# A hybrid scan and attention block: dt spread over the state groups by repeating transfers

## The reference, cut to what matters

```python
def _selective_scan(xc, dt, Bmat, Cmat, A, D):
    def step(h, inp):
        dt_t, B_t, C_t, x_t = inp
        dA = jnp.exp(dt_t[..., None] * A)                 # decay
        dBx = dt_t[..., None] * B_t[:, None, :] * x_t[..., None]   # drive = (dt * x) * B
        h = dA * h + dBx                                  # scan
        y = jnp.einsum('bdn,bn->bd', h, C_t)              # read and fold
        return (h, y)
    ...
    return jnp.swapaxes(ys, 0, 1) + xc * D

dt = jax.nn.softplus(dt_low @ W_dt + b_dt)
y = _selective_scan(xh, dt, Bmat, Cmat, A, D)
y = y * jax.nn.silu(z)
...                       # W_out, group norm, silu, + x
t = t + _L1_attn_ref(_ln_t(t), ...)      # 8 heads, 1024 x 1024 causal in the kernel's tiling
t = t + _L1_ffn_ref(_ln_t(t), ...)       # 8 experts, top 2
```

## Time and profile before

| | |
|---|---|
| median of 3 runs | 1569.61 us (1568.96 to 1571.73) |
| profiled execution, first to last instruction | 1566.7 us |
| busy: PE, DVE, ACT, POOL | 1124.4, 1171.5, 703.5, 512.5 us |
| turn 1, ring | about 73 to 146 us |
| turn 2, ring | about 200 to 274 us |
| turn 3, ring | 343 to 427 us |
| turns 4 to 8 | 427 to 1280 us, 170.6 us each |
| turns 9 to 11 | 1280 to 1567 us |

### The profile page before, as it was taken

One profiled execution on the slowest core, in us unless ns is written; L12 is line 12 of the kernel. 1 busy time (PEld: TensorE's weight loads), 2 busy tenths in 40 slices (PEclk: granted clock), 3 DMA queues, 4 the chain that ended last, 5 costly groups with the idle time before them and its releaser, 6 DMA issues. The chain is left out here.

```text
span 1566.7 us, 17517 instructions
## 1 busy us (share of the span) xinstructions
PE 1124.4 (72%) x6288; PEld 459.2 (29%) x6388; DVE 1171.5 (75%) x1391; ACT 703.5 (45%) x1298; POOL 512.5 (33%) x272
## 2 busy tenths in 40 slices
PE   1444344778877887679767887778767977796794
PEld 0111111332233333333233332333333323343342
DVE  5198189788678887788788976888778879448445
ACT  0422432337633763366534763366435651470560
POOL 2354544244424432533334432353243331000000
PEclk9666656979987899879987999789986998698995
DMA  1200150020212012111202012201212120111000
GB/s 27 60 1 14 32 111 0 21 70 1 56 41 70 1 32 65 32 45 32 52 20 70 14 24 65 72 1 31 52 25 52 32 52 8 30 32 44 3 14 7
DMA packets 25965, 55.28 MB, mean 35 GB/s; under 512 B 8582, under 2 KB 8970, under 8 KB 23499
## 3 DMA queue, kind: packets, MB, share of 16 engines
q1 hardware_dynamic: 25878, 54.15, 15.2%
HBM read 28.54 MB, written 13.00 MB: 27 GB/s over the span
## 5 line engine op out<-in xcount | busy, mean ns | idle before, releaser
L671 POOL TENSOR_TENSOR read<-state,c_rep 128x1024 f32<-128x1024 f32 x128 | 304.3, 2378 | 458.4 <-DVE state L981 430.9
L937 DVE TENSOR_REDUCE row_max<-ps 128x1 f32<-128x768 f32 (+7 forms) x384 | 349.1, 950 | 95.4 <-PE ps L1213 93.2
L812 ACT ACTIVATE probs<-ps 128x512 f32<-128x512 f32 (+3 forms) x768 | 329.4, 497 | 136.4 <-PE ps L1316 82.9
L981 DVE TENSOR_TENSOR_SCAN state<-decay,drive 128x1024 f32<-128x1024 f32 x128 | 356.6, 2786 | 1.8 <-POOL read L671 1.1
L1209 PE MATMUL ps<-k_stack,q_stack 128*128 128x512 bf16 (+3 forms) x736 | 219.7, 379 | 106.8 <-DVE row_max L937 89.2
L990 DVE TENSOR_TENSOR drive<-ps,b_rep 128x512 f32<-128x512 f32 x256 | 169.5, 676 | 105.0 <-PE ps L1247 102.2
L1313 PE MATMUL ps<-q_stack,k_stack 128*128 128x512 bf16 (+3 forms) x734 | 208.5, 343 | 38.3 <-DVE drive L990 20.0
L773 ACT ACTIVATE decay<-ps,a_scale 128x512 f32<-128x512 f32 x256 | 175.2, 696 | 117.1 <-DVE state L981 101.5
L1328 PE MATMUL ps<-probs,v_aug 128*32 128x512 f32 (+3 forms) x1536 | 169.3, 513 | 5.5 <-ACT probs L812 1.8
L1247 PE MATMUL ps<-dt_rows,pick 128*128 128x512 bf16 x224 | 103.6, 462 | 93.1 <-DVE drive L990 73.8
L1247 PE MATMUL ps<-u_rows,pick 128*128 128x512 bf16 x254 | 116.8, 460 | 47.7 <-DMA u_rows<-read 17.8
(11 more groups left out here) (172 smaller groups left out, 1236.4 us busy)
## 6 DMA issues: line engine op xcount, KB each, us to landing
q_stack<-q_parts_dram SPq DMA_DIRECT2D x48, 192.0 KB
k_stack<-k_parts_dram SPq DMA_DIRECT2D x48, 192.0 KB
dt_rows<-read SPq DMA_DIRECT2D x96, 64.0 KB, 2.0
u_rows<-read SPq DMA_DIRECT2D x96, 64.0 KB, 2.0
k_parts_dram<-read SPq DMA_DIRECT2D x40, 128.0 KB, 2.4
q_parts_dram<-read SPq DMA_DIRECT2D x24, 128.0 KB, 2.3
xs<-in_x SPq DMA_DIRECT2D x8, 256.0 KB, 3.6
residual<-in_x SPq DMA_DIRECT2D x8, 256.0 KB, 9.2
```

The costliest lines, as they stand in the source:

```text
L671: pool.tensor_tensor(read[:, k % (2 * NG), :], state[:, k % 2, :], c_rep[:, :], ALU.mult)\
L812: act.activation(probs[:, e % (2 * QUAD), 0:w], bank_of(("scores", e))[:, 0:w], ACT.Exp, scale=SCALE).then_inc(exped.sem, 1)
L937: dve.tensor_reduce(row_max[:, i, h0:h0 + nh], scores[:, :, 0:P * (i + 1)], AX.X, ALU.max, negate=True).then_inc(row_maxed.sem, 1)
L981: dve.tensor_tensor_scan(state[:, k % 2, :], decay[:, k % 2, :], drive[:, k % 3, :], 0.0, ALU.mult, ALU.add).then_inc(scanned.sem, 1)
```

## The change

dt is no longer split and replicated on PE. SP stores dt in memory (`dt_dram`, one slot per image) and reads the 8 rows of a chunk back 16 times over, once for each state, into one of two slots of `dt_spread`. ACT takes the exponential of a whole chunk of 1024 tokens from there (`decay_chunk`). The first two spreads stand ahead of u's rows on SP, the next eleven behind the row maxima, and the last three between the two groups of stacks. u keeps its three parts and its matmuls. On ACT the B copy moves ahead of the logarithm and of the group norm. The tables `UNITS_IN`, `FOLDS` and `TURNS` have a few other numbers.

```diff
-        UNITS_IN = (2, 2, 2, 1, 0, 2, 2, 0, 2, 1, 2, 1, 1, 1, 2, 1, 0, 0, 1, 1, 2, 1, 1, 2, 0, 1, 0, 1)
-        FOLDS = ((0, 0, 13), (0, 1, 13), (1, 0, 18), (1, 1, 19))
+        UNITS_IN = (2, 2, 2, 1, 0, 2, 2, 0, 2, 1, 2, 1, 1, 1, 2, 0, 0, 1, 1, 1, 2, 1, 1, 2, 0, 1, 0, 1)
+        FOLDS = ((0, 0, 12), (0, 1, 13), (1, 0, 16), (1, 1, 21))
...
+        SPREAD_FIRST = 13
...
-                    users += [(kind, k2) for k2 in units[:1] for kind in ("dt", "u")]
+                    users += [("u", k2) for k2 in units[:1]]
...
+                    def spread_dt(first, last):
+                        for k in range(first, last):
+                            if k < 2:
+                                sp.wait_ge(dt_stored.sem, dt_stored.at(c, 16))
+                            else:
+                                sp.wait_ge(decayed.sem, decayed.at(c, k - 1))
+                            hold(sp, "sp")
+                            rows = dt_dram[c.number, CH * chunk(k)[2]:CH * (chunk(k)[2] + 1), :]
+                            sp.dma_start(dt_spread[:, k % 2, :], rows.unsqueeze(0).to_broadcast([NS, CH, T]))\
+                              .then_inc(dt_spread_in[k % 2].sem, 16)
+
                     if c:
-
-                        for r, parts in enumerate((high_parts, mid_parts, low_parts)):
-                            for n, (rows, arrived) in enumerate(((dt_rows, dt_rows_in), (u_rows, u_rows_in))):
-                                sp.wait_ge(parts.sem, parts.at(c, n + 1))
-                                hold(sp, "sp")
-                                for g in range(NG):
-                                    sp.dma_start(rows[32 * r:32 * (r + 1), g, :],
-                                                 part[3 * n + r][GW * g:GW * (g + 1), :]).then_inc(arrived.sem, 16)
+                        sp.wait_ge(dt_ready.sem, dt_ready.at(c, 1))
+                        hold(sp, "sp")
+                        sp.dma_start(dt_dram[c.number, :, :], dt).then_inc(dt_stored.sem, 16)
+                        spread_dt(0, 2)
+                        for r, part_ready in enumerate((high_part, mid_part, low_part)):
+                            sp.wait_ge(part_ready.sem, part_ready.at(c, 1))
+                            hold(sp, "sp")
+                            for g in range(NG):
+                                sp.dma_start(u_rows[32 * r:32 * (r + 1), g, :],
+                                             part[r][GW * g:GW * (g + 1), :]).then_inc(u_rows_in.sem, 16)
...
+                    if c:
+                        spread_dt(2, SPREAD_FIRST)
                     if p:
-
                         sp.wait_ge(qk_parts_out.sem, qk_parts_out.at(p, 16 * 8))
                         hold(sp, "sp")
-                        for quad in range(2):
+                    for quad in range(2):
+                        if quad and c:
+                            spread_dt(SPREAD_FIRST, NJ)
+                        if p:
...
-                    for batch, work in ((c, silu_argument), (c, gate_tanh), (c, softplus_start), (p, group_norm),
-                                        (c, softplus_end), (c, take_b), (c, lambda: high(0)), (c, take_c),
-                                        (p, take_t1), (p, take_xn_t), (c, lambda: high(1)), (c, lambda: mid(0)),
-                                        (p, high_qk), (c, lambda: mid(1)), (p, mid_qk)):
+                    for batch, work in ((c, silu_argument), (c, gate_tanh), (c, softplus_start), (c, take_b),
+                                        (c, softplus_end), (p, group_norm), (c, take_c), (c, high_u), (p, take_t1),
+                                        (c, mid_u), (p, take_xn_t), (p, high_qk), (p, mid_qk)):
...
-                    def decay_unit(k2):
-
-                        k, h = k2 // 2, k2 % 2
-                        act.wait_ge(dt_rep.sem, dt_rep.at(c, k2 + 1))
+                    def decay_chunk(k):
+
+                        arrived = dt_spread_in[k % 2]
+                        act.wait_ge(arrived.sem, arrived.at(c, 16 * (k // 2 + 1)))
                         if k >= 2:
                             act.wait_ge(scanned.sem, scanned.at(c, k - 1))
+                        else:
+                            act.wait_ge(low_part.sem, low_part.at(c, 1))
                         j = chunk(k)[2]
-                        act.activation(decay[:, k % 2, halves(h)], bank_of(("dt", k2)), ACT.Exp,
-                                       scale=a_scale[:, j:j + 1])\
-                           .then_inc(decayed.sem, 1)
+                        act.activation(decay[:, k % 2, :], dt_spread[:, k % 2, :], ACT.Exp,
+                                       scale=a_scale[:, j:j + 1]).then_inc(decayed.sem, 1)
...
-                        if k2 == 0:
-                            pe.wait_ge(dt_rows_in.sem, dt_rows_in.at(c, 16 * 3 * NG))
-                            pe.wait_ge(c_copied.sem, c_copied.at(c, 1))
-                        replicate(k2, free_bank(("dt", k2)), dt_rows).then_inc(dt_rep.sem, 1)
```

93 lines of the change are left out of this document (44 added, 49 removed).

## The result

The changed kernel takes 1532.13 us (median of 4 runs, 1526.7 to 1541.07), the kernel before 1569.55 beside it; the ratio is 0.977 (95% interval 0.975 to 0.979). It is 37 us faster. The forecast was 1504 with a range of 1475 to 1540: the sign and the range held, but only 37 of 65 us came.

The account below looks back on a forecast made before the run. Handovers between engines, none of them full, were taken as the bound. From 1566.7 us came off 23.4 (front order), 8 (turn 2) and 34.2 (dt off PE): 1501.1 of span, 1504 as median, range 1475 to 1540.

Parts of the forecast that it names:

- Net 3.9 us: Fronts of turns 3 to 8: 5.6 us gained at the row maxima, 1.8 us waited at the gate; six turns, 23.4 us.
- alternation of rows 6: DVE's scan and POOL's multiply block each other: a scan takes 2.29 us alone, 3.47 if the multiply started first.
- Turn 2's step: Turn 2's front: u's split needs only its own steps, so the first drive comes 8 us sooner, between 4 and 10.
- ends at about 72, as before: 0: Turn 1: storing dt, two spreads and u's 12 transfers end at about 72, so no gain.
- Net 5.7 us a ring: Rings without dt's 32 matmuls: 8.3 us of DVE idle gone, less blocked scans; between 1 and 10, six rings 34.2 us.
- blocking term: In the ring, DVE spends part of the idle it saves blocked behind POOL; the last 1.6 shrinks to 0.35, some 1.3 goes mid-ring.
- rival A: Ring gives back almost all as PE stays longer at 1.2 GHz: only 1 us a ring, 1532 us; chance 0.22.
- The transfers: 16 spreads of 512 KB a turn land in 5.7 us (bounds 3.6 and 9.2), hidden behind the scans: 0.
- signs of being wrong: ACT waiting for dt_spread, PE's clock in the ring under 0.85, or scans closer to 3.5 us on average.
- B: Rival: rings fall to DVE's own work, 10 us each, 1478 us; chance 0.12.
- D: Rival: slow spreads bound the decay cycle; at a landing of 12 us the kernel is slower, 1650 us; chance 0.08.
- C: Rival: SP's order makes ACT wait for a spread behind the maxima or stacks, 3 us a ring, 1522 us; chance 0.10.

Follow-up runs that it names:

- front, u twice: The kernel "front" with every matmul that replicates u issued twice into its bank: 1526.41 us.
- order by turn: Changed kernel with ACT's new front order only in turns 3 to 8, the order of before in turns 1 and 2: 1526.51 us.
- u twice: Changed kernel with every matmul that replicates u issued twice into the same bank: 1529.28 us.
- without spreads: Changed kernel with only the first two of a turn's 16 spreads of dt, so its output is wrong: 1531.99 us.
- dt only: Changed kernel with ACT's front order of before (group norm, logarithm, B copy): 1544.62 us.
- tables: Changed kernel with the numbers of before in UNITS_IN, FOLDS, TURNS and DVE's list of steps: 1536.43 us.
- front: Changed kernel; in attention turns ACT does B copy, group norm, C copy, logarithm, and POOL adds the residual before making dt and u; turns 1 and 2 as before: 1516.45 us.
- the same, u twice, heads first: The kernel "front, u twice" with DVE dividing the last heads ahead of the ring's last scan: 1524.56 us.
- heads first: Changed kernel with DVE dividing the last heads ahead of the ring's last scan: 1531.97 us.

## Why the forecast was half right

**The order of the front.** Right in its mechanism: the 5.50 us stall went, the wait at the gate came (1.42, forecast 1.8). Net 3.9 us was too much; fronts of turns 5 to 8 lost 1.9 to 2.3. Two terms were missing in the step "Net 3.9 us". The gate runs beside POOL's multiply for u and is blocked by 1.07 us; the prediction's own times (the gate at 634.2, POOL making u until 635.4) put the two side by side, and its alternation of rows 6 was not applied to them. And the front begins in part at the half level, which may be 1.5 us, an estimate from the kernel "front, u twice" (fronts of 68.0 us that begin at a clock of 0.66, and 66.5 at 1.00). Against the dt change alone, whose fronts begin in the same way, the order is worth 3.4 us a front, close to what was forecast; against the kernel before it is worth nothing, where dt's cast still holds up the C copy; that this cast is the whole reason is not shown.

**Turns 1 and 2.** Turn 2's step was right: front 8.6 us shorter, 8 forecast, and the reordered table loads cost 1.6 us there, as said (order by turn: 43.7 against 45.3; one execution each, and fronts of turn 2 under one and the same order lie between 44.9 and 47.7). Its ring took back 1.2: its first two scans are blocked behind POOL's subtraction for q and k and the first multiply (3.27 and 4.41 us, where they took 2.28). For turn 1 the step "ends at about 72, as before: 0" was wrong: it gained 2.7 us, and 5 to 8 where the B copy does not come ahead of the logarithm (65.3 to 68.2 in place of 73.0). That this order holds dt back where no scores run was not seen.

**dt off PE.** This is the step that failed: "Net 5.7 us a ring", 1.4 measured in the full rings. The blocking term was right (2.6 forecast; the scans of a full ring went from 40.7 to 43.3 us, and DVE's busy time rose 3.2). The 8.3 us of idle taken away were not: 4.6 went. Each wait was priced as if PE would keep its clock. But PE's clock in the ring fell from 0.91 to 0.86 and its busy time by 4.2 instead of 8.5 us, and with the matmuls put back the ring is 2.1 us shorter at a clock of 0.95. That is rival A's mechanism, and it could be half of the 4.3 us that the ring missed. It is not shown as more than that: with the same doubling the rings of the faster kernel got longer. The rest is not settled as a term of its own, for a reason that the forecast's method could not hold: turn lengths did not move by sums of terms.

**Steps of 3.4 us.** Of the 52 periods of full turns in the 13 kernels whose POOL work is whole, 45 lie within 0.45 us of 163.85, 167.25 or 170.65. Kernels as different as the changed one, the one with u twice, the one without spreads and the one by turn settle on periods of 167.24 to 167.31. Within a period the parts move and the sum doesn't:

| kernel, mean of turns 5 to 7 | front, us | ring, us | both |
|---|---|---|---|
| before | 70.5 | 100.2 | 170.7 |
| dt only | 71.8 | 98.9 | 170.6 |
| changed | 68.4 | 98.8 | 167.2 |
| u twice | 70.6 | 96.6 | 167.2 |
| tables | 70.1 | 97.0 | 167.1 |
| front | 68.3 | 95.5 | 163.7 |
| the same, u twice, heads first | 65.0 | 98.9 | 163.9 |

So what one stretch gains the other can give back, and the price of a single term can't be read from a front or a ring alone. An edit can then show little of its worth (heads first), two halves that each give nothing give a step together, and the changed kernel's gain is one step where 9.6 us, nearly three, were forecast. In the doubled kernels the step goes with the clock at which a front begins. Elsewhere it does not: with the heads first alone all fronts from turn 4 on begin at full clock, and two periods of four are 167.3; in the kernel "front" they begin at 0.66 from turn 5 on, and three periods of four are 163.6 to 164.1. What the grant follows at that place, with the same wait ahead of it, and what holds the sum, stay open.

**The transfers.** Right: 4.5 us to landing, hidden, at 0. One sign that was to show them wrong did appear and was a bad one: ACT waits 61 us for spreads in all, in a full ring 6.5 us for the third. It is slack; that decay ends at 824.75, and DVE scans at 826.40. The other signs of being wrong stayed away (PE's clock in the ring 0.86 where under 0.85 was to tell, scans of 2.93 us on average where 3.5 was), though the ring missed most of its gain: they were set too far out. The Trainium skill, "SBUF — State Buffer", section "Who interferes with whom", lets DMA pass free beside the engines, and the kernel without spreads agrees: 97 or 22 GB/s in a ring, the same 98.9 us. The section's exclusive lock agrees too: the last scan starts at 738.58, POOL's multiply ends at 740.20, and the scan ends 2.14 us after that, at 742.34, where a free one takes 2.28. The fit of 2.0 us plus size over 436 GB/s that the prediction took from the Trainium skill stands in "DMA: Bandwidth & Descriptors", "Anatomy of one DMA", for transfers issued by GpSimd; these are issued by SP, and its 3.2 us, an estimate, fell short of the 4.5 measured.

**Rivals.** The time is A's 1532, and A's ground, PE's lower clock, was found, but that the number agrees is luck: A had 1 us a ring and the full gains elsewhere, where the rings gave 1.2 to 4.6, the fronts little over half, and turns 1 and 9 to 11 gave 2.7 and 2.2 that were in no sum. B (1478) and D (1650) are out by rows; C is out by the kernel without spreads.

## What to carry to other kernels

Before taking work off PE, ask what its clock does in the gap: here half of the removed time came back as slower matmuls. Issuing others twice is no cure by itself: it made the stage 2.1 us shorter in one kernel and 1.9 us longer in another. In a periodic pipeline look at the lengths of single turns, not at the median alone; where they fall on a few values, as here, an edit may show nothing alone and a whole step together with another. When an operation is moved ahead on one engine, follow its product through every other engine's fixed order: the same stall came back as POOL's residual, and in the first turn as a late logarithm.

## What was not expected of the hardware

POOL's multiply at a quarter of its length is worth 63 us of 1532, more than the whole change, though POOL is busy only 31% of the time; DVE's scans, which have both inputs in SBUF, took 62.9 us less in all; in turn 2 most of them went from 3.48 to 2.27 us. TensorE's granted level behind one and the same idle time of 2.18 us was 2.4 GHz in one turn and 1.2 GHz in the next, and full turns settled on 163.8, 167.3 or 170.6 us.
